# First attention of a four-layer block: its two passes interleaved unit by unit, and the mask of the maxima pass added on VectorE

## The chip, the cores and the metric

The program runs on one core of a Trainium2 chip. The metric is the time of one execution on the device, in microseconds. The core has TensorE for matrix products (PE; its loads of the stationary operand are PEld), VectorE (DVE), ScalarE (ACT), GpSimd (POOL) and SyncE (SP), which here only starts transfers. Every engine works through its own list of instructions in order and waits for the others at semaphores. TensorE reads from SBUF and writes to PSUM, 8 banks of 512 fp32 values in each of 128 partitions.

## What is computed

Four pairs of an attention and a feed-forward network, each behind a layer norm and with a residual. Only the first attention is touched. It has 8 batches of 256 queries and 256 keys, 16 heads of 16 values, and an integer mask:

```python
H = 16; NEG = -10000000000.0
qh = (q @ Wq.T + bq).reshape(B, S, H, dk).transpose(0, 2, 1, 3)     # kh, vh alike, of ctx_1024
scores = jnp.einsum('bhqd,bhkd->bhqk', qh, kh) / jnp.sqrt(jnp.float32(dk))
scores = jnp.where(mask[:, None, :, :] == 0, jnp.float32(NEG), scores)
attn = jax.nn.softmax(scores, axis=-1)
ctx = jnp.einsum('bhqk,bhkd->bhqd', attn, vh)
return ctx.transpose(0, 2, 1, 3).reshape(B, S, D) @ Wo.T + bo
```

## The kernel before

`attention0` (line 166) treats one batch after another; two heads are a unit, so a batch has U = 8 units. In the body of a batch TensorE's order is: `project` of the next batch (queries and keys, L313; values, L320), `weigh` of this batch, `scores` of the next, `spread_sums` (L384), `turn_maxima` (L347) and `output` (L391).

Each batch needs its scores twice. The first pass, `scores`, puts the scores of a unit with queries on the partitions into two PSUM banks (L338), adds the mask by a product of an identity matrix with `neg` (0 or -2^100, bf16; L340), and VectorE takes the maximum of each row (L523, one `tensor_reduce` of 1024 columns into 4). The maxima are transposed (L347) and split into parts (L457, L529, L459, L532); SP copies the parts into extra rows of `qs` (L263), so that the second product subtracts them. The second pass, `weigh`, makes the scores with keys on the partitions (L363), adds `negT` in the same way (L365), ScalarE takes the exponential (L467), and the probabilities are multiplied by V (L376), two heads of 32 columns side by side. Both passes go in turn through the same four PSUM banks, two units deep.

Precision comes from a split. Queries and keys are cut into three bf16 parts each (high L447, rest L499, middle L452, low L505), and the six products of parts that matter stand below each other in 96 rows of `qs` and `ks`, 16 rows each: the stacks. Twelve transfers each on SP's and on GpSimd's queue fill them for a batch (L228, `to_stack`). V, the projections and the output are fp32 products; the program lists two TensorE instructions for each.

A 17th column of V is 1 and yields the sums of the exponentials. VectorE takes the result out of PSUM (L541); SP lays the sums out over the partitions (L269), VectorE inverts them (L515), SP brings them back (L273), a product with `sel` spreads them (L384), VectorE multiplies (L550), the output product follows, and VectorE adds the residual (L557). `prepare` makes the masks (L493, L494) and adds V's bias (L509). All weights and the first inputs are loaded at the start by SP, and TensorE and ScalarE wait for all seven weight loads.

The first six batches run as a loop of three pairs, the last two are written out.

## Time and profile before

| | us |
|---|---|
| median of 3 runs | 2058.66 (2054.0 to 2060.04) |
| profiled execution | 2057.15 |
| its span, first to last instruction | 2055.3 |
| mean granted TensorE clock | 0.878 of full speed |
| PE busy / DVE busy / ACT busy / POOL busy | 1573.8 / 876.4 / 550.3 / 336.8 |

Times of groups overlap: a matrix product's duration contains the filling and draining of the array, so the distance between two starts, not the duration, is what a product costs in a row of many. The granted clock 1.00 is 2.4 GHz and 0.50 is 1.2 GHz; values between are mixtures over a stretch. "SPq" and "ACTq" rows are transfers being issued by an engine's queue.

### The profile page before, as it was taken

What the parts mean: (1) busy time and instruction counts of PE and PEld (TensorE: products, weight loads), DVE (VectorE), ACT (ScalarE), POOL (GpSimd) and SP (SyncE); (2) the same over time, 40 slices, a digit from 0 to 9 for tenths busy, and PEclk for the clock granted to TensorE, in tenths of its full rate; (3) what the DMA queues carried; (4) which work ended last, traced back from release to release, by engine and by line L of the source; (5) the groups of instructions that cost most, each with busy time, mean ns of one, the idle gap of its engine ahead of it and who ended that gap; (6) DMA issues with size and microseconds to landing.
All of it is one profiled execution on the core that took longest, in us unless ns stands there. A gap on an engine that the chain in (4) does not pass through costs nothing. (4 is left out here: it accounts for less than half of the span.)

```text
span 2055.3 us, 32700 instructions
## 1 busy us (share of the span) xinstructions
PE 1573.8 (77%) x11346; PEld 1345.9 (65%) x11346; DVE 876.4 (43%) x1913; ACT 550.3 (27%) x1311; POOL 336.8 (16%) x401
## 2 busy tenths in 40 slices
PE   2799997539991799999994099999999256691775
PEld 2565664429991688888874099999999244581664
DVE  5443542402224566665665011111111235448896
ACT  1233232102221455454441011111111011231553
POOL 1121120030002333332321400000000511004122
PEclk8999999569996799999995599999999678795787
DMA  4344241158132100000003454224470210101000
GB/s 127 59 76 66 48 69 12 59 200 276 39 113 86 61 7 7 7 7 2 2 1 113 148 195 148 103 67 146 148 270 18 76 47 16 34 26 41 6 15 21
DMA packets 118240, 152.13 MB, mean 74 GB/s; under 512 B 15360, under 2 KB 101376, under 8 KB 118016
## 3 DMA queue, kind: packets, MB, share of 16 engines
q1 hardware_dynamic: 101536, 123.86, 19.6%
q0 software_dynamic: 7680, 18.89, 4.1%
q10 hardware_dynamic: 8928, 8.13, 1.1%
q8 instruction: 56, 0.92, 0.2%
q14 instruction: 40, 0.33, 0.1%
HBM read 113.16 MB, written 24.64 MB: 67 GB/s over the span
## 5 line engine op out<-in xcount | busy, mean ns | idle before, releaser
L1271 PEld LDWEIGHTS f_ph<-f_xgT,f_w 128*128 128x128 f32 x3232 | 373.0, 193 | 21.7 <-issue 18.8
L1271 PE MATMUL f_ph<-f_xgT,f_w 128*128 128x128 f32 x3232 | 374.4, 277 | 16.1 <-DMA f_w<-in_f_w 14.9
L1281 PE MATMUL f_py<-f_w,f_hT 128*128 128x256 f32 x992 | 224.6, 379 | 0.0
L1281 PEld LDWEIGHTS f_py<-f_w,f_hT 128*128 128x128 f32 x992 | 183.7, 190 | 22.6 <-issue 0.2
L1342 DVE TENSOR_TENSOR f_hT<-f_ph,f_gate_o 128x512 f32<-128x512 f32 x78 | 54.0, 692 | 309.3 <-ACT f_gate_o L1305 309.3
L1376 POOL DMA_INDIRECT c_yt<-sorted_y,dest x48 | 45.6, 950 | 649.7 <-issue 648.8
L799 ACT ACTIVATE a_work<-a_ps,a_bias 128x128 f32<-128x128 f32 (+1 forms) x256 | 104.1, 419 | 149.0 <-DVE a_bias L879 91.3
L937 POOL TENSOR_TENSOR a_work<-a_work,a_recip 128x256 f32<-128x256 f32 (+1 forms) x128 | 103.1, 827 | 234.3 <-DVE a_recip L894 234.3
L145 PE MATMUL n_tp<-ident,n_xn 128*128 128x128 f32 x160 | 33.1, 384 | 134.9 <-DVE n_xn L125 134.3
L1305 ACT ACTIVATE f_gate_o<-f_ph 128x512 f32<-128x512 f32 x78 | 46.6, 597 | 295.2 <-PE f_ph L1271 295.1
L145 PEld LDWEIGHTS n_tp<-ident,n_xn 128*128 128x128 f32 x160 | 25.8, 196 | 142.7 <-DVE n_xn L125 135.9
L1260 PE MATMUL f_px<-ident,f_xg 128*128 128x128 f32 x124 | 24.3, 278 | 90.4 <-DMA f_xg<-sorted_x 90.4
L523 DVE TENSOR_REDUCE a_top_s<-a_ps 128x4 f32<-128x1024 f32 x64 | 75.7, 1215 | 16.4 <-PE a_ps L340 15.7
L899 DVE TENSOR_TENSOR a_qk<-a_ps,a_qk 128x512 fp32r<-128x512 f32 x64 | 44.3, 692 | 85.1 <-ACT a_qk L818 85.1
L467 ACT ACTIVATE a_pT<-a_ps 128x1024 f32<-128x1024 f32 x64 | 64.6, 1023 | 57.7 <-PE a_ps L365 57.7
L338 PE MATMUL a_ps<-a_ks,a_qs 96*128 96x256 bf16 x256 | 61.8, 279 | 22.3 <-DMA a_qs<-a_part 12.7
L1260 PEld LDWEIGHTS f_px<-ident,f_xg 128*128 128x128 f32 x124 | 15.7, 144 | 91.0 <-DMA f_xg<-sorted_x 91.0
L1173 POOL DMA_INDIRECT sorted_x<-xn,dest x48 | 46.4, 967 | 171.5 <-DVE dest L1149 157.5
L1349 DVE TENSOR_SCALAR f_hT<-f_ph,f_b 128x128 f32<-128x128 f32 x92 | 25.9, 345 | 111.5 <-PE f_ph L1271 111.5
L661 PE MATMUL a_ps<-a_src,a_wq_high 128*128 128x256 f32 x256 | 59.0, 312 | 17.4 <-DVE a_wk_low L843 14.6
L376 PE MATMUL a_ps<-a_pT,a_V 128*32 128x256 f32 x512 | 67.7, 385 | 2.8 <-ACT a_pT L467 1.8
L876 DVE TENSOR_REDUCE a_top_s<-a_ps 128x2 f32<-128x256 f32 (+1 forms) x128 | 64.4, 545 | 6.2 <-PE a_ps L724 6.2
(307 smaller groups left out, 3103.7 us busy)
## 6 DMA issues: line engine op xcount, KB each, us to landing
f_w<-in_f_w SPq DMA_DIRECT2D x72, 1024.0 KB, 7.2
f_xg<-sorted_x SPq DMA_DIRECT2D x62, 128.0 KB, 2.1
sorted_y<-f_yg ACTq DMA_DIRECT2D x62, 128.0 KB, 1.7
a_qs<-a_part SPq DMA_DIRECT2D x96, 64.0 KB, 5.1
a_ks<-a_part POOLq DMA_DIRECT2D x96, 64.0 KB, 5.3
sorted_x<-zeros SPq DMA_DIRECT2D x1, 4992.0 KB, 16.5
a_ctxT<-in_ctxT SPq DMA_DIRECT2D x16, 256.0 KB, 2.7
sorted_x<-zeros SPq DMA_DIRECT2D x1, 2944.0 KB, 10.2
```

Of the source, the lines that this page charges most:

```text
L145: mm = pe.transpose(tp[:, b % SLOTS, k, t * P:(t + 1) * P], xn[:, row if router else row % (SLOTS * TB), k * P:(k + 1) * P], ident[:, :])
L338: pe.matmul(bank[:, t * S:(t + 1) * S], qs[0:R, s, h, t * P:(t + 1) * P], ks[0:R, s, h, :], start=True, stop=False)
L376: mm = pe.matmul(O[W * (g0 + j):W * (g0 + j + 1), n, :], V[:, s, t, 4 * n + g0 + j, :], pT[:, m % 2, j, t, :], start=(t == 0), stop=(t == ...
L467: act.activation(pT[:, u % 2, :, :, :].rearrange("p j t n -> p j (t n)"), ps[:, 2 * (u % 2):2 * (u % 2) + 2, :], ACT.Exp, scale=float(D0) ...
L523: dve.tensor_reduce(top_s[:, :, 2 * u:2 * u + 2].rearrange("p t j -> p j t"), ps[:, 2 * (u % 2):2 * (u % 2) + 2, :].rearrange("p j (t k) - ...
L661: mm = pe.matmul(out, left[a][c], right[b][c], start=start and i == 0, stop=stop and i == len(todo) - 1)
L799: act.activation(prob[:, s, i, t * P:(P if t == 0 else TRI)], ps[:, SB + 2 * s + i, t * S:(t * S + P * (t + 1))], ACT.Exp, bias=bias[:, s, ...
L876: dve.tensor_reduce(top_s[:, s, t, :], ps[:, SB + 2 * s:SB + 2 * s + 2, t * S:t * S + P * (t + 1)], AX.X, ALU.max).then_inc(max_done, 1)
L937: pool.tensor_tensor(part, part, recip[:, s, t, :].unsqueeze(2).to_broadcast([P, 2, P * (t + 1)]), ALU.mult).then_inc(shares_done, 1)
L1271: mm = pe.matmul(ph[:, q, n, f * P:(f + 1) * P], w[:, s, k, (q * FQ + f) * P:(q * FQ + f + 1) * P], xgT[:, s, k, :], start=(k == 0), stop= ...
L1281: mm = pe.matmul(py[:, s, 0:D], hT[:, s, f, :], w2[:, s, f, :], start=(f == 0), stop=(f == FT - 1))
L1342: dve.tensor_tensor(hT[:, s, q * FQ:(q + 1) * FQ, :].rearrange("p f n -> p (f n)"), ph[:, q, 1, :], gate_o[:, q, :], ALU.mult).then_inc(h_ ...
```

## The change

- Both passes run in one stream of steps. Step k makes the scores of unit k + 9 for the maxima and the scores of unit k for the exponential, so the maxima pass is 9 units ahead (`AHEAD`), and the other work of three batches (queries, keys and values of batch i + 2, maxima of i + 1, sums and output of i - 1) is dealt out over the eight steps of batch i. All is written out, with no loop in the program.
- The second pass has PSUM banks 0 and 1, the maxima pass 2 and 3 (and 0 and 1 for odd units before the second pass starts); one unit deep each.
- Queries and keys are split into two fp32r parts, three products of parts in 48 rows. The even head of a unit stands in partitions 0 to 47, the odd one in 64 to 111; the products alternate. The host lays the weights out for this. Six transfers on each queue fill the stacks of a batch, with three batches of stacks, masks and V kept. GpSimd sets all of `ks` to 1 at the start.
- The maxima pass has no identity products. VectorE adds `neg` and takes the maximum in one instruction for each head and block of 128 queries (256 columns each), four for a unit, and writes the sums to `shut_s`.
- The second pass keeps its identity products, now before the scores, four for each unit.
- V products are made for four heads in one call, for every second unit. The transfers that turn the sums are issued by ScalarE instead of SP. Products wait only for the weights that they need.

```diff
-    PARTS = ((0, 0, 0, 1, 1, 2), (0, 1, 2, 0, 1, 0))
-    R = len(PARTS[0]) * D0
+    HALF, ROWS = P // 2, 3 * D0
+    AHEAD = U + 1
+    PARTS = ((0, 0, 1), (0, 1, 0))
+    LAND = 16 * len(PARTS[0]) * DK
+    ST, SC, OB, MB = 0, 2, 4, 6
...
-        qs, ks = sb("qs", [P, 2, H, S], BF16), sb("ks", [P, 2, H, S], BF16)
+        part = sb("part", [P, 2, 2, DK, S], F32R)
+        qs, ks = sb("qs", [P, 3, U, S], F32R), sb("ks", [P, 3, U, S], F32R)
+        shut_s = sb("shut_s", [P, 2, TB, S])
...
+        def bank(m):
+            return ST if m < AHEAD and m % 2 else SC
+        def to_stack(engine, w, n, b):
+                    for j in range(DK):
+                        engine.dma_start((qs, ks)[w][j * HALF + t * D0:j * HALF + (t + 1) * D0, b % 3, :, :].bitcast(F32),
+                                         part[:, n, w, j, :].bitcast(F32)).then_inc((q_stacked, k_stacked)[w], 16)
+        steps = range(-2 * U, B * U + 6)
...
+            def stack(b):
+                if b >= 3:
+                    sp.wait_ge(st_ready, (b - 2) * U)
+                sp.wait_ge(q_high, b + 1)
+                to_stack(sp, 0, 0, b)
+                sp.wait_ge(q_low, b + 1)
+                to_stack(sp, 0, 1, b)
+            def shift_rows(b):
+                for n in range(2):
+                    for j in range(2):
+                        row = j * HALF + ROWS + n
+                        sp.dma_start(qs[row:row + 1, b % 3, :, :].bitcast(F32), mpart[j * U:(j + 1) * U, n, :].bitcast(F32)
+                                     ).then_inc(mrow_landed, 16)
...
+            for i in range(-2, B):
+                if is_batch(i + 2):
+                    stack(i + 2)
+                if i == -2:
+                    sp.dma_start(wv[:, :, :], io["a0_wv"].rearrange("k p n -> p k n")).then_inc(v_in, 16)
+                    sp.dma_start(bv[:, :], io["a0_bv"]).then_inc(v_in, 16)
+                    load_ctx(1)
+                    sp.dma_start(wo[:, :, :], io["a0_wo"].rearrange("k p n -> p k n")).then_inc(out_in, 16)
+                    sp.dma_start(sel[:, :], io["a0_sel"]).then_inc(out_in, 16)
+                if is_batch(i + 3):
+                    load_mask(i + 3)
+                if is_batch(i + 3) and i + 3 >= 2:
+                    load_ctx(i + 3)
+                if is_batch(i + 1):
+                    shift_rows(i + 1)
...
-                            pe.matmul(bank[:, t * S:(t + 1) * S], qs[0:R, s, h, t * P:(t + 1) * P], ks[0:R, s, h, :],
-                                      start=True, stop=False)
-                            mm = pe.matmul(bank[:, t * S:(t + 1) * S], consts["identb"][:, :], neg[:, s, t, :],
-                                           start=False, stop=True)
...
+            def shut(first, which, b):
+                for j in range(2):
+                    for t in range(TB):
+                        pe.matmul(ps[:, first + j, t * S:(t + 1) * S], consts["identb"][:, :], which[:, b % 3, t, :],
+                                  start=(t == 0), stop=False, skip_group_check=True)
+            def pairs(first, left, right, rows, b, u, opens):
+                for t in range(TB):
+                        r = slice(j * HALF, j * HALF + rows)
+                        mm = pe.matmul(ps[:, first + j, t * S:(t + 1) * S], left[r, b % 3, u, t * P:(t + 1) * P],
+                                       right[r, b % 3, u, :], start=opens and t == 0, stop=True, skip_group_check=True)
+                return mm
+            def scores(k):
+                m = k + AHEAD
+                if is_unit(m):
+                    if m >= AHEAD:
+                        pe.wait_ge(max_done, m)
+                    elif m >= 2:
+                        pe.wait_ge(max_done, m - 1)
+                if is_unit(k):
+                    if k % U == 0:
+                        pe.wait_ge(neg_ready, k // U + 1)
+                    if k >= 1:
+                        pe.wait_ge(exp_done, k)
+                    shut(ST, negT, k // U)
+                if is_unit(m):
+                    if m % U == 0:
+                        pe.wait_ge(q_stacked, (m // U + 1) * LAND)
+                        pe.wait_ge(k_stacked, (m // U + 1) * LAND)
+                    pairs(bank(m), qs, ks, ROWS, m // U, m % U, True).then_inc(s_ready, 1)
+                if is_unit(k):
+                    if k % U == 0:
+                        pe.wait_ge(mrow_landed, (k // U + 1) * 64)
+                    pairs(ST, ks, qs, ROWS + 2, k // U, k % U, False).then_inc(st_ready, 1)
...
+            def weigh(b, n):
+                pe.wait_ge(exp_done, b * U + (2 * n + 2))
+                if n == 0:
+                    pe.wait_ge(v_out, b + 1)
+                    pe.wait_ge(mlo_done, b + 1)
+                    if b == 0:
+                        pe.wait_ge(ones_set, 2)
+                if n == NG // 2 and b >= 1:
+                    pe.wait_ge(o_out, 2 * b)
+                for t in range(TB):
+                    for g in range(G):
+                        mm = pe.matmul(O[W * g:W * (g + 1), n, :], V[:, b % 3, t, G * n + g, :],
+                                       pT[:, n % 2, g, t, :], start=(t == 0), stop=(t == TB - 1))
+                mm.then_inc(pv_done, 1)
...
+            for k in steps:
+                i, u = k // U, k % U
+                scores(k)
+                if u == 0 and is_batch(i + 2):
+                    queries(i + 2)
+                if u == 1 and is_batch(i + 2):
+                    keys(i + 2)
+                if u == 3 and is_batch(i - 1):
+                    spread_sums(i - 1)
+                if u in (2, 4, 6) and is_batch(i):
+                    weigh(i, u // 2 - 1)
+                if u in (4, 5) and is_batch(i - 1):
+                    output(i - 1, u - 4)
+                if u == 6 and is_batch(i + 1):
+                    turn_maxima(i + 1)
+                if u == 7 and is_batch(i + 2):
+                    values(i + 2)
+                if u == 7 and is_batch(i):
+                    weigh(i, NG - 1)
...
+            pool.memset(ks[:, :, :, :].bitcast(F32), 1.0).then_inc(set_done, 1)
...
+            def exps(k):
+                b, u = k // U, k % U
+                act.wait_ge(st_ready, k + 1)
+                if k >= 4:
+                    act.wait_ge(pv_done, k // 2 - 1)
+                act.activation(pT[:, u // 2 % 2, 2 * (u % 2):2 * (u % 2) + 2, :, :].rearrange("p j t n -> p j (t n)"),
+                               ps[:, ST:ST + 2, :], ACT.Exp, scale=float(D0) ** -0.5).then_inc(exp_done, 1)
...
+            def turn_sums(b):
+                act.wait_ge(o_out, b * 2 + 2)
+                for g in range(G):
+                    act.dma_start(sums[g * W:(g + 1) * W, :], oraw[g * W + D0:g * W + D0 + 1, :, :]
+                                 ).then_inc(sums_landed, 16)
+            def spread_rows(b):
+                act.wait_ge(recip_done, b + 1)
+                for g in range(G):
+                    act.dma_start(rrow[g * W + D0:g * W + D0 + 1, :, :], recip[g * W:(g + 1) * W, :]
+                                 ).then_inc(recip_landed, 16)
+            for k in steps:
+                i, u = k // U, k % U
+                if is_unit(k):
+                    exps(k)
+                if u == 0 and is_batch(i - 1):
+                    turn_sums(i - 1)
+                if u == 2 and is_batch(i - 1):
+                    spread_rows(i - 1)
+                if u == 0 and is_batch(i + 2):
+                    high(i + 2, 0, q_proj, q_high)
+                if u == 1 and is_batch(i + 2):
+                    high(i + 2, 1, k_proj, k_high)
+                if u == 6 and is_batch(i + 1):
+                    split_maxima(i + 1)
...
+            def low(b, n, ready, done):
+                dve.wait_ge(ready, b + 1)
+                for c in range(DK):
+                    a = dve.scalar_tensor_tensor(out=part[:, 1, n, c, :], in0=ps[:, MB + n, c * S:(c + 1) * S],
+                                                 scalar=bqk[:, n, c:c + 1], in1=part[:, 0, n, c, :],
+                                                 op0=ALU.add, op1=ALU.subtract)
+                a.then_inc(done, 1)
...
-                    dve.tensor_reduce(top_s[:, :, 2 * u:2 * u + 2].rearrange("p t j -> p j t"),
+            def maximum(m):
+                dve.wait_ge(s_ready, m + 1)
+                if m % U == 0 and m:
+                    dve.wait_ge(mt_ready, m // U)
+                if m:
+                    dve.wait_ge(max_done, m)
+                for j in range(2):
+                    for t in range(TB):
+                        a = dve.tensor_tensor_reduce(out=shut_s[:, j, t, :], in0=ps[:, bank(m) + j, t * S:(t + 1) * S],
+                                                     in1=neg[:, m // U % 3, t, :], scale=1.0, scalar=2 * NEG,
+                                                     op0=ALU.add, op1=ALU.max,
+                                                     accum_out=top_s[:, t, j, m % U:m % U + 1])
+                a.then_inc(max_done, 1)
...
+            for k in steps:
+                i, u = k // U, k % U
+                if is_unit(k + AHEAD):
+                    if (k + AHEAD) % U == 0:
+                        dve.wait_ge(neg_ready, (k + AHEAD) // U + 1)
+                    maximum(k + AHEAD)
+                if u == 0 and is_batch(i + 2):
+                    low(i + 2, 0, q_high, q_low)
+                if u == 1 and is_batch(i + 2):
+                    low(i + 2, 1, k_high, k_low)
+                if u == 1 and is_batch(i - 1):
+                    reciprocals(i - 1)
+                if u == 2 and is_batch(i + 2):
+                    prepare(i + 2)
+                if u == 3 and is_batch(i - 1):
+                    normalise(i - 1)
+                if u == 4 and is_batch(i):
+                    take_out(i, 0)
+                if u == 5 and is_batch(i - 1):
+                    residual(i - 1)
+                if u == 6 and is_batch(i + 1):
+                    split_maxima(i + 1)
+                if u == 7 and is_batch(i + 2):
+                    add_bias(i + 2)
+                if u == 7 and is_batch(i):
+                    take_out(i, 1)
```

## Rows read from the trace of the kernel before

**Rows 1.** First line of the page.

```profile
span 2055.3 us, 32700 instructions
```

**Rows 2.** Table by stretches: stretch, its us, each engine's busy time, granted clock, DMA share, GB/s.

```profile
28.50:369.80 341.30, 289.55 (x1904) 186.00 (x1904) 154.38 (x205) 97.37 (x132) 53.70 (x121) 0.94 0.37 62
...
145.85:183.28 37.43, 35.19 (x240) 22.79 (x239) 18.04 (x25) 11.69 (x16) 6.64 (x15) 1.00 0.41 65
...
332.98:369.75 36.77, 25.90 (x148) 14.59 (x148) 4.50 (x7) 8.08 (x8) 0.00 (x0) 0.81 0.01 1
```

**Rows 3.** Time line of a steady batch: start, us, engine, line, operation, count.

```profile
109.83 1.89 PE L313 MATMUL a_ps<-a_ctxT,a_wk 128*128 128x256 f32 x8
110.03 0.84 ACT L447 ACTIVATE a_part<-a_ps,a_bqk 128x256 bf16<-128x256 f32 x2 [4.67 <-PE a_ps L313]
...
117.50 0.27 PE L363 MATMUL a_ps<-a_qs,a_ks 99*128 99x256 bf16 x1
117.61 0.27 PE L365 MATMUL a_ps<-a_negT,identb 128*128 128x256 bf16 x1
117.82 1.06 PE L376 MATMUL a_ps<-a_pT,a_V 128*32 128x256 f32 x8
118.81 0.28 PE L363 MATMUL a_ps<-a_qs,a_ks 99*128 99x256 bf16 x1
...
139.31 1.88 PE L384 MATMUL a_ps<-a_rrow,a_sel 128*128 128x512 f32 x4
```

**Rows 4.** Groups by line and form: count, busy us, mean ns, idle before, releaser.

```profile
L523 DVE TENSOR_REDUCE a_top_s<-a_ps 128x4 f32<-128x1024 f32 x64 | 75.7, 1215 | 16.4 <-PE a_ps L340 15.7
...
L724 PE MATMUL a_ps<-a_qk 64*128 64x256 f32 x768 | 63.7, 299 | 0.0
...
L499 DVE SCALAR_TENSOR_TENSOR a_rest<-a_ps,a_bqk,a_part 128x256 f32<-128x256 f32 x32 | 14.0, 480 | 13.7 <-ACT a_part L447 13.7
```

**Rows 5.** Time line of TensorE in one unit of the second attention.

```profile
902.65 0.39 PE L717 MATMUL a_ps<-tri,identb 128*128 128x128 bf16 x4
902.97 0.97 PE L724 MATMUL a_ps<-a_qk 64*128 64x256 f32 x12
903.87 0.39 PE L661 MATMUL a_ps<-a_wo_high,a_o_high 128*128 128x256 f32 x1
```

**Rows 6.** Time line of ScalarE there: exponentials and their accumulator reads.

```profile
690.70 0.46 ACT L799 ACTIVATE a_work<-a_ps,a_bias 128x256 f32<-128x256 f32 x1
691.06 0.20 ACT L799 ACTIVATION_READ_ACCUMULATOR a_work<-a_ps,a_bias 128x1 f32 x1
691.15 0.36 ACT L799 ACTIVATE a_work<-a_ps,a_bias 128x128 f32<-128x128 f32 x1
```

**Rows 7.** DMA issues: by line (duration ns min/median/max), and by tile (KB, us to landing).

```profile
L269 SPq DMA_DIRECT2D a_sums<-a_oraw x32: 502/590/593, 93.2 to 352.4; - x32
...
L1319 ACTq DMA_DIRECT2D sorted_y<-f_yg x62: 337/338/412, 456.5 to 1604.5; - x62
...
a_qs<-a_part SPq DMA_DIRECT2D x96, 64.0 KB, 5.1
...
a_sums<-a_oraw SPq DMA_DIRECT2D x32, 4.0 KB, 1.7
```

**Rows 8.** Start of the attention: time line, a group, and the exponentials by line.

```profile
33.08 6.88 DVE L484 MEMSET a_ks<- 32x8192 bf16 x1 [1.76 <-issue]
...
37.35 3.35 PE L313 MATMUL a_ps<-xt,a_wq 128*128 128x256 f32 x8 [9.48 <-DMA a_ctxT<-in_ctxT]
...
57.61 0.40 PE L338 MATMUL a_ps<-a_ks,a_qs 96*128 96x256 bf16 x1 [12.74 <-DMA a_qs<-a_part]
...
L949 POOL TENSOR_TENSOR a_wo_low<-a_work,a_wo_high 128x2048 fp32r<-128x2048 f32 x1 | 4.6, 4578 | 9.7 <-ACT a_wo_high L780 9.7
...
L467 ACT ACTIVATE a_pT<-a_ps x64: 1018/1023/1024, 77.2 to 347.7; 128x1024 f32<-128x1024 f32 x64
```

**Rows 9.** Time line: the last instruction of the attention.

```profile
369.06 0.69 DVE L557 TENSOR_TENSOR x<-a_ps,x 128x512 f32<-128x512 f32 x1 [6.26 <-PE a_ps L391]
```

More of the change, by code:

```diff
@@ L408, in _, with output @@
-            project(0, 0, 0)
-            scores(0, 0, None)
-            turn_maxima(0)
-            every_batch(pe, batch)
+            def output(b, t):
+                if t == 0:
+                    pe.wait_ge(norm_done, b * 2 + 2)
+                for n in range(NG):
+                    mm = pe.matmul(ps[:, MB, t * S:(t + 1) * S], onorm[:, n, t * P:(t + 1) * P], wo[:, n, :],
+                                   start=(n == 0), stop=(n == NG - 1))
+                if t == TB - 1:
+                    mm.then_inc(wo_ready, 1)
@@ L427, in batch, with stack @@
-            def batch(b, s, half, last):
-                if not last:
-                    pool.wait_ge(pv_done, b * U + 2)
-                    stack(b + 1, 1 - s)
-            every_batch(pool, batch)
+            def stack(b):
+                if b >= 3:
+                    pool.wait_ge(st_ready, (b - 2) * U)
+                pool.wait_ge(k_high, b + 1)
+                to_stack(pool, 1, 0, b)
+                pool.wait_ge(k_low, b + 1)
+                to_stack(pool, 1, 1, b)
+            pool.memset(ks[:, :, :, :].bitcast(F32), 1.0).then_inc(set_done, 1)
@@ L434, in _ @@
+            pool.wait_ge(set_done, 1)
+            for b in range(B):
+                stack(b)
         @block.scalar
         def _(act):
-            act.wait_ge(weights, 16 * 7)
-            def split(b, first=False):
-                if not first:
-                    act.wait_ge(stacked, b * LAND + 16)
-                    act.wait_ge(k_stacked, b * LAND)
-                for n, done in enumerate((q_proj, k_proj)):
-                    act.wait_ge(done, b + 1)
-                    for c in range(DK):
-                        a = act.activation(part[:, 0, n, c, :], ps[:, 6 + n, c * S:(c + 1) * S], ACT.Identity,
-                                           bias=bqk[:, n, c:c + 1])
-                    a.then_inc(hi_done, 1)
-                for n in range(2):
-                    act.wait_ge(rest_done, b * 2 + (n + 1))
-                    act.activation(part[:, 1, n, :, :], rest[:, n, :, :], ACT.Copy).then_inc(mid_done, 1)
+            act.wait_ge(qk_in, 16 * 3)
@@ L477, in _ @@
         @block.vector
         def _(dve):
[L479 to L484 removed]
+            dve.memset(V[:, :, :, :, :], 0.0).then_inc(ones_set, 1)
             dve.memset(rrow[:, :, :], 0.0).then_inc(ones_set, 1)
[L486 removed]
+            dve.wait_ge(ones_set, 2)
```

367 lines of the change are left out of this document (119 added, 248 removed).

## Prediction

> **What bounds the kernel now.** I read the page for the span, then the table by stretches for the first attention, then the time line inside one batch. The program spans 2055.3 us [rows 1]; its profiled execution took 2057.15 us, 1.5 us under the median of 2058.66. Only the first attention changes; it lies between about 28.5 and 369.8 us, 341.3 us of the span [rows 2]. In a steady batch TensorE is busy 35.19 of 37.44 us at full clock [rows 2], so the batch is TensorE's sum. The time line shows what it is made of: two passes of eight units, each unit eight bf16 products of 256 columns, start to start 0.11 us (117.50, 117.61), so 0.89 us a unit and pass, half of it identity products that add the mask; eight instructions of probabilities by V, 0.99 us with the change of form (117.82 to 118.81); fp32 projections, eight instructions in 1.89 us, 0.235 each; the spread of the sums 1.88 us [rows 3]. DVE's eight maxima of 1.215 us [rows 4] only hold TensorE in pass 1.
>
> **The change, part by part.** I price one unit ("step"), then walk a steady batch of eight steps, then both ends.
>
> *Scores.* Two parts in fp32r, in rows 0 to 47 and 64 to 111, replace three in bf16. The second attention has this form: twelve products of 64 rows and 256 columns, alternating halves, take 0.97 us, the last 0.299 of it [rows 4, 5], so (0.97-0.30)/11 = 0.061 us from start to start. Four cost 0.245 us and end 0.24 after that. A change of form costs 0.10 us going in (902.65 to 902.97 is 0.32 for four products of 128 columns, at 0.055 each 0.22) and 0.15 coming out (902.97 to 903.87 is 0.90, less 12 x 0.061) [rows 5]. Per step: mask products of the second pass 0.445, form 0.10, first-pass scores 0.245, second-pass scores 0.245, form 0.15: 1.19 us instead of 1.78.
>
> *Maxima.* One tensor_reduce of 1.215 us becomes four add-and-maximum instructions of 256 columns with a per-partition result. None is in the trace. Nearest: the bias-add from PSUM of 256 columns, 32 in pairs, 14.0 us busy, mean 0.480 [rows 4]: a pair 0.875, so 0.395 from start to start. What the result costs is unknown. The nearest row is ScalarE's accumulator read: it moves the next instruction back by 0.09 us (691.06 to 691.15) and lasts 0.20 [rows 6]. Bounds: 0.42 (almost free) and 0.68 (0.48 whole + 0.20). I take 0.525, 0.395 + 0.13, nearer the start-to-start end since four follow each other without a wait. A step has 2.10 us of maxima where it had 1.215.
> The Trainium skill (VectorE: DVE Perf Modes, "Two Vector instructions with no wait between them") says that an op that also writes out its accumulator is two instructions. It speaks against this change; no run shown here has such an op on VectorE. Without the second instruction the price would be 0.42.
>
> *The loop of a step.* The first-pass banks are one pair (bank(m) is SC from unit 9 on), so DVE and TensorE take turns: maxima 2.10, semaphores 0.08, mask products and form 0.545, scores 0.245 + 0.24, handover: 3.27 us at least (0.06 for the two handovers). ScalarE's exponential, 1.02 us [rows 8], fits beside it.
>
> *The rest of TensorE's batch.* V products: same instruction count, four column tiles in one call instead of two. Before, 8 instructions took 0.99 against 8 x 0.235 = 1.88 untiled. hi and lo of one product follow each other on the same tile, which I think keeps the overlap at two: 16 instructions 1.9 us. If four ran side by side, 1.0. The Trainium skill (TensorE: Matmul & The Clock Gate, "Part 3: Packing small matmuls — row/col tiling") has three column tiles run 2.38 times as fast; it bears on the low bound, and no row shows more than two. Queries, keys, values 1.88 each, two output halves 1.88 each, spread 1.88, transposes 0.3. TensorE's batch: 9.5 + 5.6 + 7.6 + 1.9 + 3.8 + 0.3 = 28.7 us, so it is no longer the whole batch.
>
> *Eight steps of a steady batch.*
> Steps 0 and 1: queries done 2.4 us after the scores; ScalarE has by then started the exponential, and issues four row DMAs until 2.9 (0.59 each on SP's queue; ScalarE's own issues in the trace, of a plain block, take 0.34 [rows 7]; I take 0.59 for the same shape, and by 0.34 the whole would be about 9 us less, here and in step 3); its high part 0.84 [rows 3] until 3.7; VectorE's low part 0.875 until 4.6, its maxima until 6.7; step 2's scores are ready at 7.67. The 2 us beyond the loop is this chain. Keys' chain (5.7, 6.6, 7.6) is just inside it.
> Step 2: 3.27 (V products 1.9 fit; prepare is hidden in DVE's wait for TensorE).
> Step 3: spread waits for the reciprocal rows, 4 x 0.59 + 1.7 to land [rows 7] after the exponential's issue in step 2: about 0.9 late, 4.2.
> Steps 4 and 7: TensorE ends last: scores 0.25, form 0.15, V products 1.9, output half or values 1.88, mask and scores 0.79: 4.97 each.
> Step 5: 3.27. Step 6: transposes after the maxima, 3.54.
> Sum 31.9 us against 37.44. POOL's and SP's stacks (24 DMAs a batch, now 12 of twice the size) have six steps, about 20 us, to land; one takes 5.1 [rows 7]. The maxima rows: mlo at 0 of step 7, four issues 2.4 and 1.7 to land are 4.1, under 4.97, so step 0 does not wait. Should SP be late, each us costs one us a batch.
>
> *Start.* Projection no longer waits for all weights (37.35, behind ten loads [rows 8]); the first needs five, about 4 us earlier. Stacking shrinks from 12 issues a queue to 6. POOL must fill ks first, 6144 elements: 5.2 us at VectorE's rate (8192 in 6.88), 13.7 at POOL's (2048 in 4.58) [rows 8]; the keys' high part is ready about 41 (queries and keys at the low clock of 37.35, 3.35 us each, from 33.7), so the fill holds them by 0 to 2 us. First scores about 49 instead of 57.61. But nine units of maxima with two batches' projections between them follow (8 x 1.215 before; now 9 x 2.1 plus about 5), and then transposes, split and rows. The first exponential: about 76, against 77.2 [rows 8]. No gain.
>
> *Sum.* Batch 0 has no work of a batch before it (steps 0 and 1 are 7.1, 3 and 4 are 3.27): 28.7. Batches 1 to 5: 5 x 31.9 = 159.5. Batch 6 projects nothing: 30.2. Batch 7 has no maxima; its steps are the exponential's loop 2.4 with spread, output and V products in four of them: 23.2. Last exponential ends at 76 + 28.7 + 159.5 + 30.2 + 23.2 = 317.6, before at 347.7 + 1.0 = 348.7 [rows 8]. The end, row DMAs, spread, output and residual at half clock, took 21.1 to 369.75 [rows 9]; 21.4 with the larger last V call. New end 339.0: 30.7 us earlier. From the median 2058.7: **2028 us**; from the profiled execution 2026.4.
>
> **The rivals.**
> *Cheap end.* Four column tiles side by side (1.0) and a maximum of 0.46: steps 4 and 7 fall by 0.9, the loop by 0.26: T near 29.7; 18 us less: 2010. For it: the V products now use only 64 of the array's 128 columns. Against: in-order starts of hi and lo.
> *Dear accumulator read.* 0.68 each: the loop becomes 3.9, steps 4 and 7 stay; T 34.3; 22 us more: 2050. Still faster.
> *Slower: VectorE takes the place of TensorE.* If the two-input instruction with a result runs at half the rate of the PSUM rows, it costs another 256 elements' time, at most 0.30 by the tensor_reduce row (1.215 us for 1024), 0.27 without its fixed part: 0.80 in all: maxima 3.2, loop 4.4, T 36.4 and the nine leading units 10 us more: 44 us more, 2072. It loses to before from 0.73 per instruction on. The loop has no slack at VectorE, since scores have one pair of banks. Against: the bias-add, with one operand in PSUM and one in SBUF too, needs 0.395 to 0.48 [rows 4].
> *The clock falls.* The mean granted clock is 1.00 in the steady batch, and 0.81, a mixture of 2.4 and 1.2 GHz, in the last stretch, where TensorE is busy 25.9 of 36.8 us and waits for DMAs [rows 2]. If it fell to 1.2 GHz in steady batches, the 28.7 would double: 26 us a batch, four batches 2131. Against: TensorE is still busy about nine tenths, with no gap beyond 1.5 us.
> *It does not do what it says.* The V and output calls stack up behind each other so that the passes stay serial: within 6 us of now.
>
> **How the numbers follow.** Forecast, 2015 to 2042: 0.54. Cheap end: 0.16. Dear read: 0.12. Half-rate VectorE: 0.10. Clock: 0.04. No effect: 0.04. Faster by over 0.3% (about what a measurement can tell from no change) 0.54 + 0.16 + 0.12 = 0.82; same 0.04; slower 0.14. The first three fill 8 in 10: 2008 to 2052.
>
> **What would show it.** The groups by line: maxima x256 with a mean near 0.48 and about 0.525 from start to start, and whether a read stands behind each. The time line: 0.245 for four score products; V products x16 in 1.9 or in 1.0. The table by stretches: a steady batch of 31.9 us with TensorE busy some 0.9, clock 1.00. The waits: TensorE's first mask product waiting for the maxima in steps 1, 2, 5 and 6, none in 4 and 7; VectorE waiting for ScalarE's high part in step 0. Wrong would be: a batch over 35 us, VectorE busy above 90% of it, step 0 waiting for the rows of maxima, or a first exponential after 80 us.

## The result, and the profile after

| | before | after |
|---|---|---|
| median | 2056.57 (2050.43 to 2060.91, 10 runs) | 2070.57 (2062.0 to 2075.33, 10 runs) |
| span of the profiled execution | 2055.3 | 2070.6 |
| mean granted clock | 0.878 | 0.857 |
| end of the first attention (residual) | 369.75 | 380.93 |

The ratio is 1.0066, with a 95% interval of 1.005 to 1.0082: slower by 14 us, where 30.7 us less were predicted, and above the range of 2008 to 2052. The attention itself ends 11.2 us later; the rest of the program, from the next layer norm to the end, takes 1685 to 1695 us from one profiled execution to another. The attention was predicted to end at 339.0 and ends at 380.93, 42 us later. The table by stretches shows where these lie. The columns are those of [rows 2]; the stretches are the whole attention, three steady batches, and the last batch with its tail:

```profile
28.07:380.93 352.86, 238.37 (x1648) 149.72 (x1648) 153.91 (x627) 82.72 (x105) 32.10 (x49) 0.80 0.40 60
...
111.70:152.47 40.77, 27.57 (x207) 17.58 (x208) 19.23 (x81) 10.14 (x14) 3.36 (x6) 0.83 0.43 61
152.47:192.82 40.35, 27.96 (x207) 17.77 (x208) 18.60 (x79) 10.14 (x14) 3.31 (x6) 0.83 0.42 61
192.82:232.89 40.07, 28.34 (x207) 17.99 (x208) 18.45 (x77) 10.14 (x13) 3.31 (x6) 0.83 0.41 61
...
338.38:380.93 42.55, 28.51 (x160) 15.40 (x160) 6.22 (x10) 8.19 (x8) 0.00 (x0) 0.76 0.01 2
```

A steady batch was 37.43 us with TensorE busy 35.19 at clock 1.00 [rows 2]. Now TensorE is busy 28.34 us, some of it at half clock, and yet the batch takes 40.07, at a mean clock of 0.83. The work shrank, to the 28.7 us of the prediction and below, but TensorE now stands idle for 11.7 us of a batch where it stood 2.2. The group that carries it, on the page (busy us, mean ns, idle before):

```profile
L394 PE MATMUL a_ps<-a_rrow,a_sel 128*128 128x512 f32 x32 | 28.3, 1035 | 60.3 <-DMA a_rrow<-a_recip 49.2
```

The view of the tile `a_rrow` gives its transfers' time from issue to landing:

```profile
DMA to landing us min/median/max: 1.7/7.7/11.7
```

L394 spreads the inverted sums. In the kernel before the same view of the same tile reads "1.6/1.7/1.8". The 32 rows of the changed kernel are of two kinds: the 20 that are issued in batches 1 to 5 (numbered from 0), while the stacks of a later batch are filled, land in 7.0/10.0/11.7, and the 12 of the end, with no stack left to fill, in 1.7/1.8/1.8. In order of time, around the spread of one steady batch (start, us, engine, line, operation, count, idle before it and its releaser; the ACTq, SPq and POOL transfers are issues):

```profile
196.32 4.34 SPq L228 DMA_DIRECT2D a_qs<-a_part  x6
...
199.17 3.31 POOL L228 DMA_DIRECT2D a_ks<-a_part  x6 [37.04 <-ACT a_part L451]
199.43 0.34 DVE L561 RECIPROCAL a_recip<-a_sums 128x32 f32<-128x32 f32 x1
...
199.91 2.93 ACTq L478 DMA_DIRECT2D a_rrow<-a_recip  x4
...
201.87 0.38 SPq L244 DMA_DIRECT2D a_mask<-in_mask  x1
...
202.07 0.40 PE L330 MATMUL a_ps<-a_qs,a_ks 50*128 50x256 f32 x4
...
212.69 3.78 PE L394 MATMUL a_ps<-a_rrow,a_sel 128*128 128x512 f32 x4 [10.22 <-DMA a_rrow<-a_recip]
```

SP starts its six stack transfers at 196.32 and POOL its six at 199.17. ScalarE issues the four rows in the middle of that, by 202.84. Behind its stack SP starts three loads of 256 KB each, two masks and a context, from 201.87 on. TensorE comes to the spread at 202.5 and stands for 10.22 us; then the spread takes 3.78 us instead of 1.88 [rows 3]. The stretches of the same time, again with the columns of [rows 2]:

```profile
196.00:200.00 4.00, 3.15 (x24) 2.17 (x27) 3.61 (x14) 2.09 (x5) 0.83 (x2) 1.00 0.52 99
200.00:204.00 4.00, 2.14 (x28) 1.10 (x20) 3.31 (x18) 1.95 (x2) 2.48 (x5) 1.00 1.10 130
204.00:208.00 4.00, 0.00 (x0) 0.00 (x0) 0.00 (x0) 0.00 (x0) 0.00 (x0) 0.62 1.14 131
208.00:212.00 4.00, 0.00 (x0) 0.00 (x0) 0.00 (x0) 0.00 (x0) 0.00 (x0) 0.50 1.05 158
```

The last three numbers are the granted clock, the DMA engines' share and GB/s. The 16 DMA engines are full (1.05 to 1.14) from 200 to 212. From 204 on every compute engine is idle, and the clock goes to 0.50, the level of 1.2 GHz. The exponentials' starts show that this is one place and not a general slowness. Step 3 to step 4 of batches 1 to 5 takes 16.06, 15.69, 15.58, 14.74 and 14.74 us; in the batch from 192.82 to 232.89 the other seven distances are 3.31, 3.77, 3.04, 4.13, 3.03, 2.82 and 4.39. The three loads are not the cause: in batch 5 none follows the stack, and the rows still land in 7.0/9.8/10.1 and step 3 is as long as in batch 4.

The price of the maxima, which the prediction worried about most, came out below both its bounds. VectorE's groups by form:

```profile
L538 DVE CUSTOM_DVE_ANT_0 a_shut_s<-a_ps,a_neg 128x256 f32<-128x256 f32 x256 | 93.1, 420 | 50.4 <-PE a_ps L330 49.9
L538 DVE DVE_READ_ACCUMULATOR2_ANT a_top_s<- 128x1 f32 x256 | 21.2, 83 | 0.0
```

Three starts on its time line:

```profile
182.35 0.42 DVE L538 CUSTOM_DVE_ANT_0 a_shut_s<-a_ps,a_neg 128x256 f32<-128x256 f32 x1
...
182.69 0.42 DVE L538 CUSTOM_DVE_ANT_0 a_shut_s<-a_ps,a_neg 128x256 f32<-128x256 f32 x1
...
183.04 0.42 DVE L538 CUSTOM_DVE_ANT_0 a_shut_s<-a_ps,a_neg 128x256 f32<-128x256 f32 x1
```

Each add-and-maximum does have a read of its accumulator behind it, as the Trainium skill's rule said; but instruction and read together stand 0.345 us apart (182.35, 182.69, 183.04), not 0.525.

### The profile page after: what moved, and what is told of

Same layout as the page of the kernel before. It is cut to its first block and busy times, and to the rows that moved or that the text cites. A ratio compares the mean times of both kernels' runs of the same rounds, so it can differ in the third digit from the quotient of the medians.

```text
span 2070.6 us, 32178 instructions
## 1 busy us (share of the span) xinstructions
PE 1518.6 (73%) x11090; PEld 1306.2 (63%) x11090; DVE 873.8 (42%) x2335; ACT 536.0 (26%) x1285; POOL 315.6 (15%) x329
## 3 DMA queue, kind: packets, MB, share of 16 engines
q8 instruction: 64, 1.05, 0.2%
## 5 line engine op out<-in xcount | busy, mean ns | idle before, releaser
L460 ACT ACTIVATE a_pT<-a_ps 128x1024 f32<-128x1024 f32 x64 | 65.6, 1024 | 188.9 <-PE a_ps L330 188.9
L538 DVE CUSTOM_DVE_ANT_0 a_shut_s<-a_ps,a_neg 128x256 f32<-128x256 f32 x256 | 93.1, 420 | 50.4 <-PE a_ps L330 49.9
L1300 PEld LDWEIGHTS f_px<-ident,f_xg 128*128 128x128 f32 x124 | 15.7, 144 | 91.4 <-DMA f_xg<-sorted_x 91.4
L394 PE MATMUL a_ps<-a_rrow,a_sel 128*128 128x512 f32 x32 | 28.3, 1035 | 60.3 <-DMA a_rrow<-a_recip 49.2
L764 PE MATMUL a_ps<-a_qk 64*128 64x256 f32 x768 | 64.8, 302 | 3.5 <-issue 3.5
## 6 DMA issues: line engine op xcount, KB each, us to landing
sorted_x<-zeros SPq DMA_DIRECT2D x1, 4992.0 KB, 16.2
```

Source lines behind the costliest of these rows:

```text
L460: act.activation(pT[:, u // 2 % 2, 2 * (u % 2):2 * (u % 2) + 2, :, :].rearrange("p j t n -> p j (t n)"), ps[:, ST:ST + 2, :], ACT.Exp, sca ...
L538: a = dve.tensor_tensor_reduce(out=shut_s[:, j, t, :], in0=ps[:, bank(m) + j, t * S:(t + 1) * S], in1=neg[:, m // U % 3, t, :], scale=1.0, ...
L764: mm = pe.matmul(ps[:, SB + 2 * s + i, t * S:(t + 1) * S], qk[r, s, a, 0, t * P:(t + 1) * P], qk[r, s, b, 1, :], start=False, stop=(n == l ...
```

## The experiments

Two theories stood for the waiting rows. A: the rows share the 16 DMA engines with the twelve stack transfers, whichever queue issues them, and land only when those are nearly through. B: the cause lies with the rows themselves, in ScalarE's queue, which issues them now instead of SP's. The changed kernel's own trace already speaks for A: its last 12 rows go through the same queue of ScalarE and land in 1.8 us at most. Times are compared with runs of the kernel before on the same chip as each kernel, of median 2055.68 (the first four kernels below), 2053.36 (the next four, up to the one with identity products) and 2053.86 (the last two). Kernels of different groups are best compared by their ratios. "Layer norm" is when the next stage starts, 370.08 before and 381.25 after.

### Fewer stack bytes

```diff
-  engine.dma_start(qs|ks[.. b % 3, :, :], part[:, n, w, j, :])
+  m = 1 if b >= 3 else U                  # second kernel: 4
+  engine.dma_start(qs|ks[.. b % 3, 0:m, :], part[0:m * D0, n, w, j, :])
```

One unit of eight:

> The changed kernel, but from batch 3 on a stack transfer carries one of its eight units (16 KB instead of 128 KB), so the scores of seven units in those batches are made from old data. Theory A (the reciprocal rows wait behind the stack transfers in the DMA engines, which all queues share): the rows, issued by ScalarE, land in about 2 us instead of 7.7 (median) to 11.7, the distance of the exponentials of steps 3 and 4 falls from 16.1 to about 4, a batch from 40.3 to about 28.5 us, and five stalled batches give 60 us: about 2010. Theory B (the rows are slow because ScalarE's own queue issues and moves them, whatever else runs): landing, the 16.1 us and the time, about 2070, stay.

Four units of eight:

> The same with four of eight units (64 KB for each transfer), so four units of the later batches use old data. Theory A: the stacks keep the DMA engines for some 6.5 us instead of 13, the rows land after about 4 us, and the time lies half way, 2035 to 2045. Theory B: about 2070. If it is the number of transfers and not their bytes, it stays at 2070 while the run with an eighth stays there too.

| | time | all 32 rows land (min/median/max) | the 20 of batches 1 to 5 | step 3 to 4, batches 1 to 5 | layer norm |
|---|---|---|---|---|---|
| after | 2070.57 | 1.7/7.7/11.7 | 7.0/10.0/11.7 | 14.7 to 16.1 | 381.25 |
| four of eight | 2034.08 (one run) | 1.7/3.8/5.2 | 3.2/4.1/5.2 | 8.1 to 9.9 | 346.84 |
| one of eight | 2033.64 (one run) | 1.7/1.9/3.5 | 1.8/2.0/3.5 | 5.5 to 8.7 | 339.68 |

The landing falls with the bytes of the other queues' transfers, which A says and B doesn't. Four of eight came out 1 us under the 2035 to 2045 expected. But one eighth was expected at 2010, and the step stayed above 4. The two single runs differ by 0.4 us although the attention ends 7 us apart, which is within what the rest of the program varies by; the layer norm's start is the better measure here. The time line of one eighth shows what is left:

```profile
148.57 2.48 ACTq L479 DMA_DIRECT2D a_rrow<-a_recip  x4
...
154.03 3.78 PE L395 MATMUL a_ps<-a_rrow,a_sel 128*128 128x512 f32 x4 [2.89 <-DMA a_rrow<-a_recip]
```

TensorE was ready at 151.1. Issuing the four rows takes until 151.05 by itself, and their landing, up to 3.5, is added; then the spread runs at twice its time, as after the long wait.

### The stacks held until the rows have landed

```diff
   if b >= 3:
       sp.wait_ge(st_ready, (b - 2) * U)
+      sp.wait_ge(recip_landed, (b - 2) * (16 * G))
   ... and the same in POOL's stack(b)
```

> Everything is computed. SP and GpSimd hold the stack transfers of batch i+2 until the reciprocal rows of batch i-1 have landed. Theory A: rows land in 2 us, the stall of 12 us in step 3 goes; the stacks then have from step 3 to step 7, about 14 us, for their 13 us, so TensorE may wait up to 3 us at step 7: a batch 29 to 32 us, 2010 to 2025. Theory B: rows as late as before and stacks later still: 2085 or more.

It took 2030.01 us (2025.59 to 2041.87), 0.9885 of before (0.9837 to 0.9934): some 40 us less than the changed kernel, though 5 above the 2010 to 2025 expected, with every byte moved and ScalarE's queue as it was. The rows land in 1.7/1.8/2.6, the layer norm starts at 337.68, 43.6 earlier than after. So A is shown and B falls. A steady batch by stretches, and the spread of the next one in order of time:

```profile
142.48:173.84 31.36, 27.06 (x207) 17.29 (x208) 18.68 (x79) 10.14 (x14) 3.15 (x6) 0.95 0.53 78
```

```profile
184.56 3.18 PE L395 MATMUL a_ps<-a_rrow,a_sel 128*128 128x512 f32 x4 [1.07 <-DMA a_rrow<-a_recip]
```

A batch takes 31.36 us. TensorE still waits 1.07 us for the rows and spreads in 3.18. And the stacks now land late: from step 6 to 7 it is up to 5.7 us, where 2.82 stood. SP's three loads, which follow its stack in its list, are held with it.

### The spread two steps later

```diff
-  if u == 3 and is_batch(i - 1): spread_sums(i - 1)      # VectorE: normalise
+  if u == 5 and is_batch(i - 1): spread_sums(i - 1)
-  if u in (4, 5) and is_batch(i - 1): output(i - 1, u - 4)
+  if u in (6, 7) and is_batch(i - 1): output(i - 1, u - 6)
-  if u == 7 and is_batch(i + 2): values(i + 2)            # add_bias too
+  if u == 3 and is_batch(i + 2): values(i + 2)
   ... take_out(i, 0) at step 5, residual at step 7
```

> Everything is computed. The spread of the sums moves from step 3 to step 5, output to steps 6 and 7, values to step 3; transfers are issued when they were. Theory A: rows still take about 10 us to land, but two steps, 6 us, hide most of it: a stall of 4 to 6 us stays in step 5, a batch about 34 us, 2030 to 2045. Theory B gives the same here, since it too has rows that land 10 us after their issue; this run prices the stall and not its cause.

2038.67 (2032.77 to 2045.53), ratio 0.992 (0.9887 to 0.9953). The rows land as late as before the edit (1.7/7.4/11.5), and step 5 to 6 now holds the wait: 9.0 to 10.2 us where some 3 stood. The excess is 6 to 7 us instead of about 11, so two steps hide some 5 us of it, not all, as Theory A had it. With the hold as well:

> Both edits at once: the stacks of batch b wait until the rows of batch b-3's sums have landed, and the spreading, normalising, output and residual steps come two steps later (values and their bias at step 3). In the kernel with the hold alone TensorE still waited about 1.1 to 1.9 us a batch for the rows and then spread at a lower granted clock (3.18 to 3.78 us instead of 1.9). Theory A (what is left after the hold is the rows' own issue and landing, about 4.5 us after the reciprocals): two steps more give the rows over 6 us, the wait and the slow spread go, 2 to 4 us in each of 8 batches: 2000 to 2020 against 2030 with the hold alone. Rival: the two later output steps meet the step with the transposed maxima and the values of the second pass, and the stacks, held as before, are waited for at step 7: 2028 to 2040.

2035.89 (2032.26 to 2043.98), ratio 0.9918 (0.9887 to 0.9949): the expected gain is absent, and the rival's 2028 to 2040 holds. The rows are no longer waited for; the stacks are. In order of time:

```profile
187.82 1.99 PE L394 MATMUL a_ps<-a_rrow,a_sel 128*128 128x512 f32 x4
...
198.70 0.80 PE L331 MATMUL a_ps<-a_ks,a_qs 48*128 48x256 f32 x4 [4.21 <-DMA a_qs<-a_part]
199.30 0.63 PE L331 MATMUL a_ps<-a_qs,a_ks 50*128 50x256 f32 x4
199.86 3.78 PE L401 MATMUL a_ps<-a_wo,a_onorm 128*128 128x256 f32 x8
```

The spread is at full clock (1.99), but the first product of the next batch waits 4.21 us for its stack, and the output half behind it takes 3.78, twice its time.

### The start in another order

```diff
   sp.dma_start(wv ...); sp.dma_start(bv ...)
+  sp.wait_ge(q_stacked, LAND); sp.wait_ge(k_stacked, LAND)
   load_ctx(1); wo; sel; load_mask(1)
+  (step -1: wait for batch 1's stacks, maxima rows first, then load_mask(2), load_ctx(2))
```

> The hold of the stacks, and the start in another order: context, mask, Wo and sel loads of SP (1.5 MB) wait until batch 0's twelve stack transfers have landed, and batch 2's masks and context until batch 1's have. Theory (the shared DMA engines also set the start: the first scores at 55.5 and the first exponential at 84.4 in the kernel with the hold alone wait for stacks that share the engines with those loads): first scores at 48 to 51, first exponential at 74 to 79, whole kernel 2020 to 2026 against 2030. Rival (the stacks' own transfers, 1.57 MB for each batch, set their landing, not the loads beside them): first scores within 1.5 us of 55.5 and the later loads make the values and keys late: 2030 to 2036.

2030.49 (2028.39 to 2033.0), ratio 0.9883 (0.9841 to 0.9924), as with the hold alone. The first scores came at 53.82, not 48 to 51, and the first exponential at 82.54 where the hold alone had 84.43. Six us of this kernel in which only the stacks, wv (256 KB) and bv (128 KB) are under way:

```profile
44.00:50.00 6.00, 0.00 (x0) 0.00 (x0) 0.00 (x0) 0.00 (x0) 0.00 (x0) 0.50 1.10 152
```

The DMA engines are full (1.10) although the other loads have not begun. The 152 GB/s are a mixture, since up to 0.39 of the 0.91 MB are wv and bv. The stacks by themselves can be read in batch 5 of the changed kernel, where no load follows them:

```profile
279.00:283.00 4.00, 2.22 (x28) 1.13 (x24) 3.39 (x18) 1.96 (x2) 2.56 (x5) 1.00 1.17 125
283.00:287.00 4.00, 0.00 (x0) 0.00 (x0) 0.00 (x0) 0.07 (x1) 0.00 (x0) 0.56 1.11 129
```

12 transfers of 128 KB are 1.57 MB, some 12 us at 125 to 129 GB/s. The loads held back here cost 1.7 us, not 5. With the later steps too:

> All three edits: hold, later steps, start in another order. If they are independent, the gains add: about 2030 minus 10 to 25 for the later steps and minus 4 to 10 for the start, 1998 to 2015. If the start's gain is lost later (the first batches wait for masks, context or Wo that now come later), it equals the kernel with hold and later steps within 3 us.

2041.3 (2029.33 to 2044.04, median of 7; an eighth took 6046.15 and is not counted), ratio 0.993 (0.9907 to 0.9953). Neither the sum of gains that was expected is there, nor is the time within 3 us of the 2035.89 without this edit, though the two intervals overlap. In the trace its layer norm starts at 341.84 against 343.94. Neither edit touches the wait for the stacks at step 7 (8.2 to 9.5 us from step 6 to 7).

### The mask of the maxima pass by identity products again

```diff
+  pe.wait_ge(neg_ready, m // U + 1)
+  shut(bank(m), neg, m // U)
-  pairs(bank(m), ..., True)
+  pairs(bank(m), ..., False)
-  four tensor_tensor_reduce of 256 columns
+  dve.tensor_reduce(top_s[:, :, :, m % U] ..., ps[:, bank(m):bank(m) + 2, :] ..., AX.X, ALU.max)
```

> The hold of the stacks, but the maxima pass adds its mask as the kernel before did, by four bf16 identity products into the score banks, and VectorE takes the maxima of a unit with one tensor_reduce (1.2 us). Everything is computed. This is the other half of the change undone. TensorE gets 0.53 us more in each of 64 steps; a step that is set by the round of scores and maxima goes from 0.53 + 0.34 + 4 x 0.345 + hand-overs to 1.06 + 0.34 + 1.2 + hand-overs, about 0.4 us longer. Theory (the adding and maximum on VectorE is worth about that): 2048 to 2064 against 2030 with the hold alone. Rival (the steps wait for batch work and transfers, and the mask products fall into that waiting): 2028 to 2036. Second rival (the busier TensorE holds its clock and gains): below 2026.

2045.14 (2037.44 to 2050.13), ratio 0.9955 (0.9936 to 0.9975), against 0.9885 with the hold alone. So, with the stacks held, the mask on VectorE is worth some 14 us, by ratios whose intervals just miss each other, and all the rest of the change together (the interleaving, the fp32r stacks, the V products for four heads, the start) some 8 to 9; what the interleaving is worth by itself no run shows. The traces agree on the first: the end of the attention moves by 16.9 (layer norm 354.54 against 337.68). The 2048 expected at least is missed by 3. In order of time:

```profile
153.03 0.61 PE L324 MATMUL a_ps<-a_negT,identb 128*128 128x256 bf16 x4 [0.17 <-DVE a_top_s L540]
153.48 0.60 PE L324 MATMUL a_ps<-a_neg,identb 128*128 128x256 bf16 x4
...
154.83 1.16 DVE L540 TENSOR_REDUCE a_top_s<-a_ps 128x4 f32<-128x1024 f32 x1
```

TensorE pays 0.45 us more in a step (153.03 to 153.48), and VectorE's 1.16 to 1.22 instead of 4 x 0.345 = 1.38 give only 0.2 of it back. That leaves 0.25 us a step, 16 us for 64 steps, an estimate near the 16.9.

### Only the k stacks held

Against the kernel with both stacks held:

```diff
   POOL's stack(b): wait_ge(recip_landed, (b - 2) * (16 * G)), as above
-  SP's stack(b):   the same wait
```

> Only POOL's six k transfers wait for the rows of batch b-3's sums; SP's six q transfers go as in the changed kernel. Everything is computed. Theory A (all transfers share the DMA engines, whichever queue issues them): half of the stack bytes are still ahead of the rows, so the rows land like those of the kernel with half the bytes, 3 to 5 us, and exponentials 3 to 4 stand 8 to 10 us apart; but the stacks are complete some 5 us earlier than with both held, so the steps 6 to 7 and 7 to 0 fall from 5.6 and 4.1 to 5.8 back to 2.8 and 4.4: 2028 to 2040, as with half the bytes or a little above. Rival (only POOL's software queue delays the rows): rows land in under 2.6 us, exponentials 3 to 4 about 4 apart, 2010 to 2024. Second rival (only SP's queue does, since its stack is issued right ahead of the rows): rows land in 7 us or more, 2050 to 2070.

2035.4 (2031.2 to 2043.42), ratio 0.9908 (0.9873 to 0.9944), rows landing 1.7/4.1/5.1 (3.8/4.3/5.1 in batches 1 to 5), step 3 to 4 8.2 to 9.8 us, step 6 to 7 back at 2.82. That is the kernel with half the bytes once more, as expected: taking POOL's six transfers away halves the landing and does not end it, so neither queue alone is to blame, but what is in front in the DMA engines. SP's three loads still follow its stack here, and the rows land in 5.1 at most.

The same wait on POOL alone, together with the spread two steps later, as in the diff above:

> POOL's k transfers held as before, SP's q transfers free, and the spreading, normalising, output and residual two steps later. With both stacks held and the later steps, the rows were no longer waited for, but the stacks landed late: exponentials 6 to 7 stood 8.3 to 9.3 us apart and 7 to 0 5.8 to 6.5, where 2.8 and 4.4 are free of it. Theory A: with half of the bytes sent ahead the k stack alone needs some 6 us less after the rows, so that excess of 8 us a batch falls to 0 to 3, and the rows, 3 to 5 us in landing, fit into the two later steps: 2000 to 2018. Rival (POOL's k transfers, 8.8 us in landing against 4.5 for q, are by themselves what is late at step 7): 6 to 7 stays above 7 us and the time within 2028 to 2038.

**2005.44** us (2001.65 to 2014.26, 5 runs), ratio 0.9749 (0.9725 to 0.9773): 2.5% faster than the kernel before, the best of all. It needs both edits, and their gains add: from the changed kernel's ratio of 1.0066 the later steps alone take 1.5 points, the k hold alone 1.6, and both 3.2. The profiled execution took 2014.26. Its stretches, the attention and two steady batches:

```profile
28.07:317.07 289.00, 226.27 (x1648) 145.89 (x1648) 151.61 (x627) 82.60 (x105) 31.19 (x49) 0.88 0.44 73
164.78:192.01 27.23, 25.60 (x207) 16.98 (x207) 18.62 (x80) 10.12 (x13) 3.14 (x6) 1.00 0.52 90
192.01:219.46 27.45, 25.30 (x206) 16.75 (x206) 18.14 (x78) 10.12 (x14) 3.15 (x6) 1.00 0.49 90
```

In order of time:

```profile
168.28 4.35 SPq L228 DMA_DIRECT2D a_qs<-a_part  x6
...
172.04 2.48 ACTq L478 DMA_DIRECT2D a_rrow<-a_recip  x4
...
178.29 3.14 POOL L228 DMA_DIRECT2D a_ks<-a_part  x6 [23.62 <-DMA a_rrow<-a_recip]
...
180.24 1.98 PE L393 MATMUL a_ps<-a_rrow,a_sel 128*128 128x512 f32 x4
```

The three kinds of transfers are issued one after the other: q stack from 168, rows from 172, k stack from 178. The rows still meet the end of the q stack and land in 3.8 to 4.4 us in this batch, not 1.7, but the two later steps cover that. The spread at 180.24 waits for nothing and takes 1.98 us, the clock is 1.00, and a batch takes 27.2 us, 10 less than before the change. The k stack is late by 1.1 us at most: step 6 to 7 takes 4.25 to 5.38 us, against 4.25 to 4.33 with the later steps alone.

## Why the prediction was wrong

**The step that failed** is the one that priced step 3: "spread waits for the reciprocal rows, 4 x 0.59 + 1.7 to land", about 0.9 late, 4.2 us in all. Measured are 15.58. The other seven distances of that batch sum to 24.49 us where the prediction had 27.7, so no other term was too low in sum. Over batches 1 to 5 step 3 took 76.8 us instead of 21.0, 55.8 more, and all other steps 122.8 instead of 138.5, 15.7 less: 199.6 us, 40.1 over the 159.5 predicted. The two errors pull in opposite directions: with step 3 as priced and all else as measured the attention would have ended some 14 us before the predicted 339.0 (an estimate, 380.93 less 55.8).

It had two halves. The 1.7 us was read from rows that travel alone. In the kernel before, the same rows follow the stacks in SP's own list. The table by stretches of the kernel before, in the batch of [rows 2], shows it, with SP's issues below:

```profile
150.00:155.00 5.00, 4.78 (x37) 3.37 (x36) 2.77 (x5) 3.11 (x5) 4.88 (x11) 1.00 0.99 150
155.00:160.00 5.00, 5.00 (x43) 2.57 (x41) 0.00 (x0) 2.72 (x3) 1.76 (x5) 1.00 1.14 127
160.00:165.00 5.00, 5.00 (x44) 2.86 (x40) 0.69 (x1) 2.39 (x3) 0.00 (x0) 1.00 0.42 43
165.00:170.00 5.00, 4.45 (x38) 2.49 (x36) 2.25 (x3) 1.02 (x1) 0.00 (x0) 1.00 0.01 1
```

```profile
148.36 7.74 SPq L228 DMA_DIRECT2D a_qs<-a_part  x12
168.18 2.48 SPq L269 DMA_DIRECT2D a_sums<-a_oraw  x4
172.34 2.45 SPq L273 DMA_DIRECT2D a_rrow<-a_recip  x4
```

The DMA share is 0.99 and 1.14 for ten us, and 0.01 from 165 to 170; SP issues the sums at 168.18 and the reciprocals' rows at 172.34. After the change ScalarE issues the rows at 199.91, 3.6 us behind SP's first stack transfer and 0.7 behind POOL's. The second half is that the stacks were weighed only as something that may be late ("six steps to land; one takes 5.1"), never as traffic that others wait behind. Yet the traffic is about the same: the shares of the DMA engines sum to 15.2 us from 145 to 165 before, loads included, and to 16.2 from 196 to 214 after. The Trainium skill (DMA: Bandwidth & Descriptors, "Issuing engines are not separate DMA queues") says that transfers started by ScalarE, SyncE or GpSimd all run on the same 16 DMA engines and interleave; the trace agrees on the sharing, though here the small rows landed at the end of the large transfers (7.5 to 10.6 us in the batch from 192.82) rather than in between.

**The wait's second price** was the clock. The prediction had it as a rival at 4 in 100, with "no gap beyond 1.5 us" against it. Once there was a gap of 10 us the granted clock was 0.50, and the work behind ran at half speed: 3.78 for the spread instead of 1.88, 1.9 us a batch, not the 26 of that rival, since the clock came back within the step (1.00 from 220 to 222).

**Terms mis-sized, mechanism right.** Maxima: 0.345 us from start to start, not 0.525, and below the lower bound of 0.42, which the bias-add pair of two operands had set. V products: 16 instructions in 1.07 us (189.89), so the four column tiles do overlap, the cheap bound of 1.0:

```profile
189.89 1.07 PE L379 MATMUL a_ps<-a_pT,a_V 128*32 128x256 f32 x16
```

Together these are the "cheap end" rival's mechanism, at 0.16. In the last kernel, where the stall is gone, a batch is 27.2 us and the time 2005, where that rival had 29.7 and 2010 (its own terms, 2 x 0.9 and 4 x 0.26 off 31.9, give about 29). That is near by luck in part: the last kernel has two edits that the prediction's had not, and its first exponential comes at 82.13, not 76.

Step 4 was 4.13 and step 7 4.39, not 4.97; a light step 2.8 to 3.0, not 3.27; steps 0 and 1 together 7.08, not 7.67 (whose "2 us beyond the loop" are 1.1 by the prediction's own numbers, 7.67 less 2 x 3.27). Right were the mask and score products of a step, 1.20 us from start to start (194.54 to 195.74) for the 1.19 predicted, a projection or output half, 1.83 for 1.88, ScalarE's issue of a row, 0.62 (2.47 for four) for 0.59, and VectorE's wait for ScalarE's high part in step 0 (2.83 us at 196.28).

**The signs of being wrong.** The batch was over 35 us (40.07), and the first exponential came after 80 (86.11). Step 0 did wait for the rows of maxima, but for 0.44 and 0.34 us in two batches only (151.92 and 192.28). VectorE was busy 18.45 of 40.07 us, far from 90%.

**The start** was expected at 49 for the first scores and 76 for the first exponential; it was 55.05 and 86.11:

```profile
55.05 0.79 PE L330 MATMUL a_ps<-a_ks,a_qs 48*128 48x256 f32 x4 [16.50 <-DMA a_ks<-a_part]
...
79.90 0.79 PE L330 MATMUL a_ps<-a_ks,a_qs 48*128 48x256 f32 x4 [3.96 <-DMA a_ks<-a_part]
```

The cause is the same: both waits are for the k stack. The other suspect is cleared: GpSimd filled `ks` from 28.72 to 33.94, 5.22 us, the lower of the two prices, and began to issue the k stack at 40.13. Issues fell from 12 a queue to 6, but 1.57 MB is what it was, and the transfers, not their issuing, set the landing. These are 10.1 us of the error. Adding up: the start +10.1, batch 0 -3.1, batches 1 to 5 +40.1, batch 6 -3.1, batch 7 +0.7, the tail -2.8 (18.6 instead of 21.4), together 41.9, the 380.93 for 339.0.

**Not settled.** Why the rows land after nearly all the stack bytes, and not in turn with them, was not tried apart. Fewer stack bytes were also fewer packets, so the runs don't tell which of the two the rows wait for. Nor was it tried whether the rows would do better on another queue, SP's as before among them, with the stacks in flight.

## What to carry to other kernels

A transfer's landing time belongs to the traffic beside it: before a small transfer on the critical path is moved to another queue or another time, look at the DMA share of the stretch into which it moves, and count the bytes in flight there. Where an engine's list used to put small after large or large after small, that order may have been a protection (the old kernel issued its rows when the share of the engines was 0.01), and a move needs a wait in its place. Large transfers that have slack can be split around the small one, some ahead and some behind, and its reader moved later by what it still waits; here the two together turned 0.66% slower into 2.5% faster, and either alone gave about half of that.

## What the runs showed of the hardware

- Four rows of 4 KB, issued while twelve transfers of 128 KB on two other queues were in flight, landed in 10.0 us (median of 20; 7.0 to 11.7) instead of 1.7 to 1.8, and in 9.8 in the batch in which no load followed the twelve; with only SP's six ahead of them in 4.3; with twelve of half the size in 4.1, with twelve of an eighth in 2.0.
- Twelve stack transfers alone, 1.57 MB between SBUF tiles, ran the 16 DMA engines at a share of 1.11 to 1.17 with 125 to 129 GB/s, so they need some 12 us.
- Add-and-maximum on VectorE, 256 fp32 columns from PSUM with a bf16 mask from SBUF and a result per partition: 0.345 us from start to start in a row, its own read of the accumulator (83 ns) included; four of them, 1.38, are close to one plain tensor_reduce of the same 1024 columns, 1.22.
- After TensorE had waited 2.89, 4.21 or 10.22 us, the next four or eight products took 3.78 us instead of 1.88 to 1.99. After shorter waits it was one or the other: in the kernel with both stacks held the spread took 3.39 us after a wait of 1.93 and 3.18 after one of 1.07, but 1.98 after one of 1.12 and after one of 1.94 in the next two batches.
